# Colour weights ahead of the grey taps, and a new written order of the first four steps, in a one-core vision layer

## The reference, cut to what matters

```python
gray  = einsum('bchw,c->bhw', x, (0.2989, 0.587, 0.114))      # x: 64 x 3 x 256 x 256, f32
edge  = abs(conv3x3(gray, scharr)).sum(over the 2 filters) / 2  # 'SAME'
h  = edge
n  = layernorm(h)                    # over the row, 256 wide; the rows are the tokens
xs = n shifted down by one row
xk, xv, xr = n*tm + xs*(1-tm)        # three mixes
k, v, r = xk @ Wk.T, xv @ Wv.T, xr @ Wr.T
h  = h + (sigmoid(r) * wkv(w, u, k, v)) @ Wo.T   # wkv: a recurrence over the rows
n2 = layernorm(h)
e  = argmax(n2 @ Wg.T)               # one of 8 experts for each row
h  = h + gelu((layernorm(n2)*s_e + b_e) @ W1_e + b1_e) @ W2_e + b2_e
```

## Time and profile before

| | |
|---|---|
| median of three runs | 1105.36 us (1104.49 to 1108.51) |
| profiled execution | 1103.89 us |
| its span | 1102.2 us, 17860 instructions |
| busy: PE, DVE, ACT, POOL | 1065.7, 1025.5, 987.7, 274.8 us |
| mean granted clock of PE | 0.989 |
| step 6 (the loop) begins | PE 143.35 us, DVE 149.26 us |
| a turn of the loop | 31.9 us |

### The profile page before, as it was taken

How to read it: one execution, slowest core, us unless ns; L and a number is a source line. 1 busy time by engine, 2 the same in 40 slices (tenths; PEclk the granted TensorE clock), 3 DMA queues, 4 the chain that set the end, 5 groups by cost and what they waited for, 6 DMA issues and landing times.

```text
span 1102.2 us, 17860 instructions
## 1 busy us (share of the span) xinstructions
PE 1065.7 (97%) x6139; PEld 777.9 (71%) x6139; DVE 1025.5 (93%) x1875; ACT 987.7 (90%) x1581; POOL 274.8 (25%) x292
## 2 busy tenths in 40 slices
PE   7885999999999999999999999999999999999997
PEld 3463767777777777777777777777777787777875
DVE  5896999999999999999999999999999999999950
ACT  1677899999999999999999999999999999998872
POOL 4211123332212333221233322222333221230001
PEclk9997999999999999999999999999999999999999
DMA  8787888999899889999888999899999998873223
GB/s 176 172 164 150 157 135 153 164 177 192 168 151 164 163 155 184 183 178 151 156 165 162 176 176 186 165 149 164 159 166 179 188 169 147 167 104 77 39 39 39
DMA packets 177218, 168.30 MB, mean 153 GB/s; under 512 B 13794, under 2 KB 177184, under 8 KB 177184
## 3 DMA queue, kind: packets, MB, share of 16 engines
q1 hardware_dynamic: 125970, 118.74, 49.0%
q0 software_dynamic: 50048, 48.25, 34.7%
q10 hardware_dynamic: 1166, 0.89, 0.4%
HBM read 102.80 MB, written 80.76 MB: 167 GB/s over the span
## 4 chain that ended last, share of the span: by engine, by line
PE 90%; ACT 4%; DMA 3%; DVE 2%; issue 1%; SPq 0%; POOL 0%; POOLq 0%; DVEq 0%
PE bank L1926 24%; PE bank L2101 20%; PE bank L2040 15%; PE bank L1964 10%; PE bank L2025 10%; PE bank L1935 5%; PE bank L1972 2%; DMA gray_dram<-planes 2%; PE bank L1947 2%; PE bank L2102 1%; PE bank L2055 1%; PE bank L2065 1%; DMA rows_in<-gray_dram 1%; ACT hidden L1429 1%; DVE max_state L613 0%
## 5 line engine op out<-in xcount | busy, mean ns | idle before, releaser
L2101 PE MATMUL bank<-w_sb,hidden 128*128 128x256 f32 x1024 | 239.1, 380 | 2.5 <-ACT hidden L1429 2.4
L473 POOL DMA_DIRECT2D out_dram<-moe x64 | 76.3, 1192 | 605.5 <-ACT moe L1441 586.0
L2101 PEld LDWEIGHTS bank<-w_sb,hidden 128*128 128x128 f32 x1024 | 184.6, 190 | 31.4 <-ACT hidden L1429 3.9
L1964 PE MATMUL bank<-rows_in,conv_w 102*32 102x512 f32 x960 | 112.1, 607 | 8.3 <-DMA rows_in<-gray_dram 8.2
L2025 PE MATMUL bank<-w_o_t,den 128*128 128x256 f32 x512 | 117.8, 383 | 1.2 <-DVE den L671 1.2
L2040 PE MATMUL bank<-normed_hi,w_hi 128*128 128x512 f32 x256 | 109.8, 429 | 0.0
L2025 PEld LDWEIGHTS bank<-w_o_t,den 128*128 128x128 f32 x512 | 94.8, 190 | 14.3 <-issue 2.6
L2040 PE MATMUL bank<-normed_lo,w_hi 128*128 128x512 f32 x256 | 101.0, 394 | 0.0
L2040 PE MATMUL bank<-normed_hi,w_lo 128*128 128x512 f32 x256 | 100.9, 394 | 0.0
L613 DVE TENSOR_TENSOR_SCAN max_state<-neg_exp_w,bank 128x256 f32<-128x256 f32 x128 | 80.5, 671 | 11.0 <-PE bank L1926 10.7
L598 DVE SCALAR_TENSOR_TENSOR mixed_vr<-normed,params,normed_t 128x512 f32<-128x512 f32 x128 | 90.2, 747 | 0.1
(11 more groups left out here) (170 smaller groups left out, 2672.3 us busy)
## 6 DMA issues: line engine op xcount, KB each, us to landing
rows_in<-gray_dram SPq DMA_DIRECT2D x180, 256.0 KB
planes<-in_x_dram SPq DMA_DIRECT2D x120, 256.0 KB, 8.1
gray_dram<-planes POOLq DMA_DIRECT2D x120, 256.0 KB, 5.7
out_dram<-resid SPq DMA_DIRECT2D x64, 256.0 KB, 4.6
out_dram<-moe POOLq DMA_DIRECT2D x64, 256.0 KB, 5.3
gray_dram<-in_x_dram SPq DMA_DIRECT2D x60, 256.0 KB, 4.9
rows_in<-gray_dram SPq DMA_DIRECT2D x120, 24.0 KB
rows_in<-in_x_dram SPq DMA_DIRECT2D x6, 256.0 KB
```

The source lines that it names most:

```text
L473: pool.dma_start(out_rows(at.j, at.u - FFN, half), moe[:, 2 * half:2 * half + 2, :], accum_op=ALU.add).then_inc(added[half], 16)
L1964: ins = pe.matmul(bank[BANK_EDGE[n]][ROW_TILE * q:ROW_TILE * (q + 1), :], conv_w[0:TAPS, c, :], rows[:, q, :, :].rearrange("p i w -> p (i ...
L2101: pe.matmul(ps, hidden[:, m, i, rows], w2_sb[:, m, :], start=(m == 0), stop=False)
```

## The change: what it does

First, in DVE's set-up the colour weights `color_w` are built before the taps of the grey convolution (`scharr_dj`). The scaled filter gets a place of its own in `conv_w`, which is written over later; before, it was scaled in place, so the grey taps had to be taken from it earlier. `clear_outside(1)` stands before the grey taps now.

```diff
             dve.wait_ge(s_scharr_all_in, 16)
+            scaled = conv_w[0:TAPS, :, :].rearrange("p c r -> p (c r)")[:, 0:18]
+            done(dve.tensor_scalar(scaled, scharr_all[0:TAPS, 0:18], shade[0:TAPS, :], 0.5, ALU.mult, ALU.mult))
+            dve.wait_ge(s_cleared, CLEARED_TAPS)
+            for di in range(3):
+                weights = scaled.rearrange("p (c di dj) -> p c di dj", c=2, di=3)[:, :, di, :]
...
+            for b in range(1, 2):
+                clear_outside(b)
             for dj in range(3):
                 ins = dve.tensor_scalar(scharr_dj[ROW_TILE * dj:ROW_TILE * (dj + 1), :],
...
-            done(dve.tensor_scalar(scharr_all[0:TAPS, :], scharr_all[0:TAPS, :], shade[0:TAPS, :], 0.5,
-                                   ALU.mult, ALU.mult))
```

Second, the written orders of `first_steps` are new on DVE, ACT and PE, with the waits that belong to them, and the products without use stand at other places: 22 (5, 3, 3, 3, 4, 4) where there were 24 (6, 3, 2, 6, 5, 2). A few lines of it:

```diff
                 scale_first_layer()
+                low_weights(1)
+                low_weights(0)
+                dve.wait_ge(s_normed_t[0], 1)
...
-                pe.wait_ge(s_abs[0], 1)
-                keep_busy(bank[BANK_NORMED[1]], 6)
+                pe.wait_ge(s_abs[3], 1)
+                keep_busy(bank[BANK_EDGE[3]], 5)
+                pe.wait_ge(s_abs[3], 1)
+                pe.wait_ge(rows_loaded[1], 160)
+                convolve(3, EDGE, pair(1, EDGE), waits=False)
                 pe.wait_ge(s_normed, 1)
```

More of the change, by code:

```diff
@@ L552, in _ @@
                 clear_outside(b)
+            for dj in range(3):
+                ins = dve.tensor_scalar(scharr_dj[ROW_TILE * dj:ROW_TILE * (dj + 1), :],
+                                        scharr_all[ROW_TILE * dj:ROW_TILE * (dj + 1), dj:18:3],
+                                        0.5 * GRAY_WEIGHTS[2], None, ALU.mult)
+            for n in range(6):
+                rows, dj = slice(3 * ROW_TILE, TAPS - n), 2 - n % 3
+                dve.tensor_scalar(scharr_dj[rows, :], scharr_all[rows, dj:18:3], 0.5 * GRAY_WEIGHTS[2], None,
+                                  ALU.mult).then_inc(s_edges_w, 1)
+                dve.wait_ge(s_edges_w, n + 1)
             for di in range(3):
@@ L1550, in first_steps @@
                 act.preload_act_table_set("natural_log_exp_and_others")
-                act.wait_ge(s_edge_ps[0], 1)
+                act.wait_ge(s_pe_setup, 1)
+                copy_params()
+                act.wait_ge(s_pe_setup, 2)
+                high_weights(1)
+                act.wait_ge(s_pe_setup, 3)
+                high_weights(2)
+                absolute(1, EDGE, pair(0, EDGE), waits=False)
+                act.wait_ge(s_pe_setup, 4)
+                high_weights(0)
+                absolute(2, EDGE, pair(0, EDGE), waits=False)
                 absolute(0, EDGE, pair(0, EDGE), waits=False)
@@ L1678, in first_steps @@
+                absolute(0, EDGE, pair(3, EDGE), waits=False)
+                absolute(3, EDGE, pair(3, EDGE), waits=False)
                 absolute(2, EDGE, pair(3, EDGE), waits=False)
-                act.wait_ge(s_mix_v, 3)
-                high_v(EDGE, pair(2, EDGE), waits=False)
+                act.wait_ge(s_v_ps[0], 3)
+                copy_v(0, WKV, pair(2, WKV), waits=False)
                 act.wait_ge(s_gap[0], 3)
+                decay_arg(WKV, pair(2, WKV), waits=False)
+                bonus_of(WKV, pair(2, WKV), waits=False)
@@ L1682, in first_steps @@
+                act.wait_ge(s_decay_arg, 3)
+                decay_of(WKV, pair(2, WKV), waits=False)
                 fresh_arg(WKV, pair(2, WKV), waits=False)
-                bonus_of(WKV, pair(2, WKV), waits=False)
-                decay_arg(WKV, pair(2, WKV), waits=False)
+                act.wait_ge(s_v_ps[1], 3)
+                copy_v(1, WKV, pair(2, WKV), waits=False)
+                act.wait_ge(s_mix_r, 3)
+                high_r(WKV, pair(2, WKV), waits=False)
+                act.wait_ge(s_route_ps, 1)
@@ L1706, in first_steps @@
-                act.wait_ge(s_hidden_ps[3], 1)
-                gelu(3, FFN, pair(0, FFN), waits=False)
-                gelu(0, FFN, pair(0, FFN), waits=False)
                 act.wait_ge(s_normed_ps[0], 4)
@@ L1712, in first_steps @@
                 copy_normed(1, EDGE, pair(3, EDGE), waits=False)
+                gate_of(0, WKV, pair(2, WKV), waits=False)
                 act.wait_ge(s_shift[1], 2)
```

434 lines of the change are left out of this document (199 added, 235 removed).

## The result

The changed kernel takes 1098.49 us in the median of five runs (1096.16 to 1100.95), the kernel before 1104.49 (1104.11 to 1108.51): ratio 0.9939, 95% interval 0.9924 to 0.9953. Timed again later beside other kernels the ratio was 0.9941 (0.9920 to 0.9961). The profiled execution took 1098.49 us, its span is 1096.9 us.

What follows compares the result with a forecast made beforehand. PE was taken to set the loop's turns and DVE, the fuller engine, the steps before it. Gains of 7.6 and 2.7 us less 3.0 at the start gave 7.3 off 1103.89: 1096.6, said as 1097 us; range 1090.5 to 1104.

Steps and rivals of the forecast that it cites:

- What bounds: Whole kernel: PE alone sets the loop's 31.90 us turns, so the change is worth what it moves the loop's beginning.
- Rival (3): Loop from step 6: entered out of phase, PE waits each turn; with 0.8 us a turn 1117 us; chance 0.08.
- Start: Up to DVE's first L678: PE waits for pair 1's pixels, so L678 comes at 36.0, 3.0 us later.
- the row's 29.2: Landing of pair 1's pixels, taken from pair 0's pixels, seen 2.8 us after their bytes had moved.
- Colour weights bring nothing: Start: weights ready near 8.4 instead of 12.2, but no gain, since pair 1's pixels are late next.
- 33 to 86 us: DVE there: two low_weights (1.4 us) leave the path, idle falls from 2.8 to 1.5; gain 2.7 us.
- The hole: 86 to 149.3 us: a 7.3 us wait from queue order goes, 1.5 us of waits stay; gain 7.6 us.
- Rival (2): 86 to 149.3 us: pair 3's grey chain slips 3 to 4 us; 1100 to 1101 us; chance 0.13.
- past 95.5 every microsecond reaches `best_logit`: Rival (2)'s claim that any landing of pair 3's rows after 95.5 us delays DVE's best_logit equally.
- No DVE wait over 3 us: Sign of the forecast: DVE has no wait over 3 us between 36 and 142 us.
- Sum: All terms, 7.6 + 2.7 - 3.0: 7.3 us off the profiled 1103.89, giving 1096.6; said as 1097.

Runs made afterwards that it cites:

- e1: Kernel before with only the set-up part of the change, colour weights ahead of the grey taps, all old orders kept: 1103.97 us, ratio 0.9994.
- e3: Changed kernel with the transposes of pair 0's normalised rows put ahead of pair 1's first convolution on PE: 1096.95 us, ratio 0.9922.
- e4: Kernel before with only PE's order changed: pair 0's second transposes and logits ahead of pair 3's convolutions and their wait: 1100.36 us, ratio 0.9954.
- e2: Changed kernel with DVE's old set-up, grey taps first and colour weights last: 1095.58 us, ratio 0.9918.
- second trace: Profile of the unaltered changed kernel when timed again: profiled execution 1096.35 us, ratio 0.9941.
- first trace: Profile of the changed kernel at its first measurement against the kernel before: profiled execution 1098.49 us, ratio 0.9939.
- c0: The changed kernel, unaltered, timed and profiled again against the kernel before: ratio 0.9941, profiled execution 1096.35 us.
- e9: Changed kernel with seven more products without use on PE, around pair 2's transposes and ahead of pair 0's logits: ratio 0.9935.
- e6: Changed kernel with both scalings of pair 3 and copy_router earlier in ACT's order: ratio 0.9923.
- e8: Changed kernel with transpose_logits on PE behind the first convolution of pair 3 instead of the third: ratio 0.9926.
- e5: Changed kernel with 13 instead of 5 products without use on PE ahead of the wait for pair 1's pixels: ratio 0.9910.

## Why the prediction was right, point by point

**What bounds.** Right for the loop: 954.5 us from step 6 on in every kernel but for 0.3 us, turns of 31.90. Rival (3), a longer turn, did not occur in any of the thirteen traces.

**Start: 3.0 us lost, 3.15 measured; the moments right, the meaning not.** L678 was forecast at 36.0 and came at 36.13, the pixels at 29.2 and came at 28.62, the first quarter of pair 1 was to take 4.4 us and took 5.33. The 2.0 us of fixed cost that the Trainium skill gives ("DMA: Bandwidth & Descriptors", "Anatomy of one DMA — SWDGE (gpsimd) path") led to 28.4; the page has it for DMAs issued by gpsimd, and SP issued these. In eight traces with this order on SP, PE saw these pixels between 28.46 and 29.43. That is later than the page's 28.4 in all eight, and later than the row's 29.2 in four. No run shows on how many DMA engines the small DMAs of three colours ran, so why the tail is as long as it is stays open. The ratio of 4.66 to 2.78 for a low clock was taken from one row, and 5.33 is the half clock for the whole of it.

What failed is the price of an early start. The sum took a microsecond at pair 0's L678 for a microsecond at the end, because "DVE does the whole work of four pairs almost without a stop". That holds for a late L678: in the nine traces with the changed order (convolution ahead of transposes) pair 1's L678 stands 16.99 or 17.00 us behind pair 0's, whether the pixels, the clock or DVE's own queue had set the first. It does not hold for an early one: e1 puts L678 5.14 us earlier and nothing comes of it, e3 5.5 us earlier and 2.4 are left, since PE's convolutions of pair 1, that is pixels and clock, then set pair 1. Of the 3.15 us late at pair 0, 1.35 are left at pair 1. That 3.0 was met so closely is in part luck: against e4, whose start is that of the kernel before, it is 1.6 us at pair 0, and at pair 1 the changed kernel is 0.2 us ahead.

**Colour weights bring nothing.** Right, and for the reason given; e1 (0.9994) and e2 (no loss without them) show it. The ratio of e2 is even the lower one, with intervals that overlap.

**33 to 86 us: 2.7 gained, 3.19 measured from pair 0's L678 to pair 2's** (2.16 in the second trace). 1.8 of it falls between the first two L678: the two `low_weights` and `rates`, which took DVE 1.7 us there (38.03 to 38.75, 40.08 to 41.07), stand ahead of the first one now, as forecast (1.4, without `rates`). PE's 5.56 us wait at 62.49 was not foreseen. DVE has work of its own there; the granted clock falls (0.72 in 60 to 72, 0.57 in the second trace).

**The hole: 7.6 forecast; 5.20 in the first trace, 8.39 in the second.** That the 7.3 us were an order of queues is shown by e4. What the step left out is the clock: it let PE work pair 3's rows at full speed, as c0 does and the first trace does not. It also had the rows at 95.5 instead of 97.2: the scaling ended 1.34 us later than before, SP issued the rows' DMAs 2.68 us later and they landed 2.8 us later. Rival (2) foresaw a slip of this size, and its sentence "past 95.5 every microsecond reaches `best_logit`" is refuted by c0: the rows are as late there, at 97.03, and `best_logit` does not wait. They cost something only where DVE gets there earlier, 1.32 us in e9. "No DVE wait over 3 us" held in the second trace and not in the first.

**Sum.** 3.15 - 3.19 - 5.20 = -5.24 us in the first trace, 3.12 - 2.16 - 8.39 = -7.43 in the second; forecast were -7.3. Most of the difference between the first trace and the forecast is the clock in the hole. The forecast's 1097 lies between the two medians, 1098.49 and 1096.59.

## What to carry to other kernels

Price an earlier start at the engine that next waits for a transfer, not at the engine that is fullest on average: 5 us gained at 28 us were gone by 52, since another pair's pixels and PE's low clock stood between. Where a wait is for a DMA that only later work needs, look at what stands behind it in the queue; moving that ahead was here worth about 5 us. And profile the unaltered kernel twice before crediting an edit with a wait that has gone.

## What was not expected of the hardware

An idle of PE of about the same length sometimes halves its clock and sometimes not, in the same program. Before pair 2's transposes it was 2.10 us in the first trace of the changed kernel, and the granted clock was 0.59 from 86 to 90; it was 2.08 us in the second, and it was 1.00. The windows 78 to 84 above don't explain it, since the idle itself begins inside the first one, at 83.3 us, and behind the second, at 84.7; up to there PE was busy without a stop and at clock 1.00 for more than 11 us in both. Nor does the length of an idle tell what it costs. At the start of the kernel before, pair 0's 96 rows took 12.18 us after 4.04 us of idle, and 13.66 us after 2.94 us in e4, the same program up to there. The 24 rows of pair 1's first quarter took 5.33 us after 3.84 (e9), 4.34 and 4.46 us (the changed kernel), but 4.47 after 4.62 (e6) and 4.96 after 4.99 (e8), and the full-speed 2.78 after 1.26 (e5). What decides it stays open.

The low clock outlasts the idle. Behind the 5.56 us of idle at 62.49 PE was busy without a stop, and the clock was still 0.50 from 62.5 to 68.5 us in the first trace and from 62.5 to 71.5 in the second. Each microsecond of work at the low clock costs half a microsecond, and eight products on zeros bought 2.2 us at pair 1.
